# Two Newton halves moved from the opening of an audio tower into its token groups

## What is computed

```python
fr = jnp.fft.rfft(xp, axis=-1)
feats = jnp.concatenate([jnp.abs(fr), jnp.angle(fr)], axis=-1)
h = jax.nn.gelu(feats @ W1 + b1, approximate=False) @ W2 + b2

inv_term = jnp.linalg.inv(I - 0.5 * dt * A)        # 32 x 32
A_bar = (I + 0.5 * dt * A) @ inv_term
# scan: state = tanh(state @ A_bar.T + ub_t)        (state space layer, on layernorm(h))
# scan: z, r, c gates; h_new = z * h + (1 - z) * c  (recurrence, 256 wide, 320 steps)
```

## Time and profile before

| | us |
|---|---|
| median of 3 runs | 890.94 |
| lowest, highest | 890.02, 891.04 |
| the profiled execution | 889.93 |
| its span | 888.1 |
| PE busy | 831.7 (94%) |
| DVE busy | 583.0 (66%) |
| ACT busy | 370.9 (42%) |
| POOL busy | 74.5 (8%) |
| half clock on TensorE in the front | 54.0 to 67.65 |

### The profile page before, as it was taken

How to read it: one execution, slowest core, us unless ns; L and a number is a source line. 1 busy time by engine, 2 the same in 40 slices (tenths; PEclk the granted TensorE clock), 3 DMA queues, 4 the chain that set the end, 5 groups by cost and what they waited for, 6 DMA issues and landing times.

```text
span 888.1 us, 40652 instructions
## 1 busy us (share of the span) xinstructions
PE 831.7 (94%) x17111; PEld 704.6 (79%) x17111; DVE 583.0 (66%) x3495; ACT 370.9 (42%) x2016; POOL 74.5 (8%) x189
## 2 busy tenths in 40 slices
PE   8999999989999999999999999999999998988875
PEld 7677667778888888888888888888888887877765
DVE  5343538376777776767767777777677777676655
ACT  5565766433343443433434434334334343343322
POOL 3111102110000000100000001000000000000000
PEclk9979999955555555555555555555555555555555
DMA  7100000000000000000000000000000000000000
GB/s 172 38 1 0 1 1 1 2 3 3 7 3 6 7 3 6 7 3 6 4 6 7 3 6 7 3 6 4 7 6 4 6 7 3 6 6 3 7 3 8
DMA packets 7454, 8.53 MB, mean 10 GB/s; under 512 B 1343, under 2 KB 6557, under 8 KB 7271
## 3 DMA queue, kind: packets, MB, share of 16 engines
q1 hardware_dynamic: 6965, 5.92, 2.9%
q0 software_dynamic: 256, 0.01, 0.0%
q10 hardware_dynamic: 50, 0.00, 0.0%
HBM read 4.62 MB, written 1.31 MB: 7 GB/s over the span
## 4 chain that ended last, share of the span: by engine, by line
PE 85%; ACT 7%; DVE 4%; issue 3%; POOL 0%; POOLq 0%; DVEq 0%
PE ps L1527 42%; PE ps L1533 11%; PE ps L1340 8%; PE ps L1238 4%; PE ps L1440 3%; PE ps L1541 3%; PE ps L1404 3%; DVE h_hi L479 2%; PE ps L1448 2%; ACT addend L847 1%; PE ps L1322 1%; PE ps L1329 1%; PE ps L1310 1%; PE ps L1260 1%; PE ps L1254 1%
## 5 line engine op out<-in xcount | busy, mean ns | idle before, releaser
L1527 PE MATMUL ps<-h_hi,w_first 128*128 128x8 f16 x2552 | 267.6, 170 | 27.8 <-DVE h_hi L479 27.7
L1527 PEld LDWEIGHTS ps<-h_hi,w_first 128*128 128x128 f16 x2552 | 220.3, 104 | 89.8 <-DVE h_hi L479 89.8
L1527 PE MATMUL ps<-h_hi,w_rest 128*128 128x8 f16 x5104 | 275.8, 168 | 0.0
L1527 PEld LDWEIGHTS ps<-h_hi,w_rest 128*128 128x128 bf16 x5104 | 241.0, 105 | 0.1
L837 ACT ACTIVATE tanh_r<-ps 128x16 f32<-128x16 f32 x320 | 59.2, 185 | 250.2 <-PE ps L1533 249.7
L1533 PE MATMUL ps<-h_lo,w_first 128*128 128x8 f16 x2560 | 159.0, 168 | 0.1
L1527 PE MATMUL ps<-rh_hi,w_first 128*128 128x8 f16 x1276 | 136.0, 172 | 12.6 <-DVE rh_hi L1132 0.9
L1527 PEld LDWEIGHTS ps<-rh_hi,w_first 128*128 128x128 f16 x1276 | 109.0, 104 | 39.6 <-DVE rh_hi L1132 1.1
L1527 PE MATMUL ps<-rh_hi,w_rest 128*128 128x8 f16 x2552 | 138.6, 168 | 0.0
L479 DVE TENSOR_TENSOR_SCAN h_hi<-coef,addend 128x32 f16<-128x32 f32 x320 | 73.3, 229 | 83.7 <-ACT addend L847 83.7
L1527 PEld LDWEIGHTS ps<-rh_hi,w_rest 128*128 128x128 bf16 x2552 | 121.2, 105 | 0.0
(11 more groups left out here) (210 smaller groups left out, 1375.3 us busy)
## 6 DMA issues: line engine op xcount, KB each, us to landing
x_sb<-in_x SPq DMA_DIRECT2D x4, 500.0 KB
out<-res SPq DMA_DIRECT2D x20, 64.0 KB, 2.0
W_sb<-in_L_tok_W SPq DMA_DIRECT2D x1, 606.0 KB
W_sb<-in_L_tok_W SPq DMA_DIRECT2D x1, 384.0 KB
wnat<-in_L_ffn_Wwr SPq DMA_DIRECT2D x1, 256.0 KB, 5.5
wnat<-in_L_ffn_Wwz SPq DMA_DIRECT2D x1, 256.0 KB, 11.8
wnat<-in_L_ffn_Ww SPq DMA_DIRECT2D x1, 256.0 KB, 10.4
wunat<-in_L_ffn_Wur SPq DMA_DIRECT2D x1, 128.0 KB, 7.1
```

Source lines behind the costliest of these rows:

```text
L1527: mm(gate(c, j, g, m), w[:, m * 128:(m + 1) * 128], state[:, k * NB:(k + 1) * NB], start=False, stop=False, skip_group_check=True)
```

## The change

`EARLY` goes from 8 to 6: halves 6 and 7 leave the opening, and with them 24 fillers. `WARM` goes from 52 to 47. The places are dealt anew: the first place of groups 0 and 1, (0, 0, 0) and (1, 0, 0), is left free, and in groups 1 and 3 slot 1 of the last two pieces is used. The wait for the second imaginary part, which the loop of the opening had, moves to the half in place (0, 0, 1). From group 4 on each half stands where it stood.

```diff
-WARM = 52
+WARM = 47
 BUSY = 6
-EARLY = 8
+EARLY = 6
...
         def blocked(n, m, slot):
-            if slot == 1 and n % 2:
+            if slot == 1 and n % 2 and (n > 3 or m < MC - 2):
                 return True
...
-            if (n, m, slot) in ((0, SQRT_PIECE + 2, 1), (2, SQRT_PIECE + 1, 1), (4, SQRT_PIECE + 1, 1)):
+            if (n, m, slot) in ((0, 0, 0), (1, 0, 0), (0, SQRT_PIECE + 2, 1), (2, SQRT_PIECE + 1, 1), (4, SQRT_PIECE + 1, 1)):
                 return True
...
             a.activation(biasT[:], bank(6)[:, 0:32], ACT.Copy).then_inc(su_act, 1)
-            for i in range(6, EARLY):
-                newton(i)
...
             tr(bank(6)[:, 0:32], bias_rows[:], ident[0:32, 0:32]).then_inc(bias_psum, 1)
-            for i in range(6, EARLY):
-                if i == 6:
-                    pe.wait_ge(im_read, 2)
-                busy(2 * BUSY if i == 6 else BUSY, 7)
-                newton(i)
-            busy(BUSY, 7)
             pe.wait_ge(w1_in, 32)
...
                     i = SLOTS[n, m, slot]
+                    if (n, m, slot) == (0, 0, 1):
+                        pe.wait_ge(im_read, 2)
```

## The result

The changed kernel took 887.46 us in the median of six runs (887.05 to 887.83), the kernel before beside it 891.01 (890.02 to 892.71): a ratio of 0.9957, 95% interval 0.9945 to 0.9968. It is faster by 3.6 us, 0.4%, where 9.6 from the median were forecast. The range held the time, by 0.04 us and only because it reached to rival 2; the sum behind the forecast did not come out.

The account below looks back on a forecast made before the run. PE was taken to bound the front, through needless work, waits and lower clock. Terms -0.55 - 3.12 - 1.33 - 5.37 + 1.2 = -9.2 gave 880.7 from the profile, 881.8 from the median; forecast 881.3, range 879.0 to 887.5.

Parts of the forecast that it names:

- rival 2: A lower-clock stretch remains, at group 1's head, its table-load wait or the opening: 886.1 or 886.7 us; chance 0.26.
- (d): Group 1: with the 1.48 us wait cut to about 0.5, the clock stays up; -5.37 us, bounds 0 and -5.9.
- (b): Opening's end: 24 fillers and halves 6 and 7 go, first angle product starts earlier; -3.12 us, bounds -2.6 and -3.2.
- The third place: Group 1's wait for the table loads, 1.13 us by group 3, named as a place where the clock could fall.
- (a): Program start: five fillers fewer, so first patch transposes start earlier; -0.55 us, bounds 0 and -0.69.
- (c): Group 1's head: Newton place left free, so the output product starts with its gelu; -1.33 us, wait 0.4 to 0.6 left.
- The twin: Group 3, same products as group 1 at full clock: 15.81 us against 21.18, used to price the lower clock.
- (e): Ends of groups 1 and 3: four more Newton halves at 0.30 each; +1.2 us, bounds 0.8 and 2.8.
- Rival 3: Clock falls at group 1's table-load wait and doesn't come back soon: +23, some 904 us; chance 0.08.
- Rival 4: Two lower-clock stretches of the old length: 891.4 us, no change; chance 0.05.
- Rival 5: Opening: something the fillers hid makes PE wait, so the start and opening gains come back: 884.4 us; chance 0.07.
- a stretch at 0.50 ahead of 160 us: Half granted clock anywhere ahead of 160 us; the prediction named this as showing it wrong.

Follow-up runs that it names:

- e5: The changed kernel itself, measured again with nothing altered, on another chip: 885.26 us, 0.9937 of the kernel before.
- e3: Changed kernel with the Newton place at group 1's head taken again and the added place at that group's sixth piece free; short opening stays: 887.04 us, 0.9975.
- e4: Changed kernel with the 52 warm-up transposes of the kernel before instead of 47, nothing else: 883.82 us, 0.9935.
- e8: Changed kernel with three and four fillers in the opening's later waits for halves 7 and 8, the bias-column wait left empty: 883.44 us, 0.9926.
- e14: Changed kernel with four fillers in the 0.54 us wait at group 1's head, opening's wait left empty, run once more: 882.66 us, 0.9929.
- e2: Kernel before with only the Newton place at group 1's head freed, one place at that group's last piece taken for it: 882.82 us, 0.9923.
- e1: Changed kernel with eight filler transposes in the opening's 0.93 us wait for the bias columns: 881.84 us, 0.9913.
- e16: Kernel before with twelve fillers in the 1.48 us wait at group 1's head, no place moved: 884.84 us, 0.9947.
- e13: Changed kernel with eight fillers in the opening's bias-column wait and four in the wait at group 1's head: 882.32 us, 0.9919.
- e15: The changed kernel itself, measured a fourth time with nothing altered: 885.09 us, 0.9945 of the kernel before.
- e6: Changed kernel with eight fillers and half 6 in the opening's bias-column wait, the added place at group 1's sixth piece free again: 882.62 us, 0.9913.
- e11: Changed kernel with four fillers in the 0.54 us wait at group 1's head, opening's wait left empty: 882.73 us, 0.9917.
- e10: Changed kernel with eight fillers in the opening's bias-column wait, the same kernel as e1 run again: 883.38 us, 0.9932.
- e12: The changed kernel itself, measured a third time with nothing altered: 885.84 us, 0.9953 of the kernel before.

## Why the prediction came out wrong

**The step that failed** is the last sentence of (d)'s first half, "So I take it that the clock stays up", together with the cover in (b). (b) priced what the fillers and halves 6 and 7 had covered as 1.19 us of waiting that costs nothing, and put no price on an empty PE. (d) then looked for the one place as empty as the 1.48, found 1.13 and 0.88 without a fall in one profile, and took that for safe. The same opening with a wait of 0.93 fell in three of the changed kernel's four profiles and held in the fourth, e5, and in e3, e4, e8 and e14; the wait of about 0.5 at group 1's head, which (d) took as harmless, fell in e5 (0.53) and held in the ten other profiles that have it, e2 and e4 among them. So at these lengths a fall is no property of the wait alone: it comes in some executions and not in others, and one profile shows one of them. Behind the 1.48 it looks certain: all 47 executions of the kernel before beside e1 to e16 have a mean clock of 0.591 to 0.593, that of its profile. Rival 2, with two of its three places named rightly, is what happened, at 886.1 to 886.7 forecast and 887.46, 885.26, 885.84 and 885.09 measured; it deserved more than 0.26. That the range held the time is this rival's doing, and luck: its lower end, 879.0, is not the sum that it names, which gives 889.93 - 10.18 = 879.75. The third place, the wait behind the arctangents (0.78 to 0.93 in group 1, 1.13 in group 3), fell in no profile.

The sizes, by steps:

- (a) five fillers fewer, -0.55 forecast. -0.69 in the first pair of profiles, but that can't be put down to the change. With 52 warm-up transposes the first patch transposes start at 9.59, 8.74, 9.65 and 9.17 (before, e2, e4, e16), 9.29 in the mean; with 47 at 8.90 to 9.75 in fourteen profiles, 9.29 in the mean. A late rise of the clock makes the same warm-up longer (rise at 5.30, patch transposes at 8.90; at 7.67, 9.75), and with an early one PE waits for DVE's odd halves (0.92 in e5, to 9.33). The lower bound, 0, was right, for other reasons.
- (b) -3.12 forecast, -3.03 from the first patch transposes to the first angle product (in e4 -3.12). The rows of the bias columns carried it: from the bias transpose to the first angle product 2.65 was forecast and 2.66 measured; PE's idle part of it was 0.93, not 1.19.
- (c) -1.33 forecast, -1.31 measured, with the wait of 0.54 that was forecast at 0.4 to 0.6.
- (d) -5.37 forecast. By e16, which has group 1 as before and at full clock, 21.18 - 16.44 = -4.74. The twin was not quite one. Group 1's wait behind the arctangents is 0.78, not group 3's 1.13; and in group 1 the even half stands ahead of the angle product and in group 3 the odd one, so a piece takes 2.03 in the one (e16, group 1, the first three rows) and 1.79 in the other (the kernel before, group 3):

```profile
55.80 0.65 PE L1238 MATMUL ps<-magT,W_sb 101*128 101x256 f32 x2
56.45 0.41 PE L1254 MATMUL ps<-Xn,step_w 128*128 128x32 f32 x2
...
57.83 0.65 PE L1238 MATMUL ps<-magT,W_sb 101*128 101x256 f32 x2
...
99.65 0.68 PE L1238 MATMUL ps<-magT,W_sb 101*128 101x256 f32 x2
100.17 0.36 PE L1256 MATMUL ps<-DY 128*128 128x64 f32 x2
...
101.44 0.68 PE L1238 MATMUL ps<-magT,W_sb 101*128 101x256 f32 x2
```

- (e) +1.2 forecast; 17.17 - 16.44 = 0.73 in group 1, 16.54 - 15.81 = 0.73 in group 3, and 0.22 in the rest of group 0, which no term had: +1.68, inside its bounds.

With these sizes and no fall the sum is -3.03 - 1.31 - 4.74 + 1.68 = -7.4, and e4, whose profile has no fall, shows it: 157.76 from the first patch transposes to the first `tanh_r`, against 165.26 before, -7.50. From a kernel before at 889.8 to 891.1 this is 882.3 to 883.7; the fastest execution of the changed kernel on each of the three later chips is 882.12, 882.94 and 883.63 (the last with 3.41 us at half clock). The rest is the falls: in the changed kernel's profiles that way takes 162.32, 161.41, 161.00 and 159.59, so 4.6, 3.7, 3.2 and 1.8 above e4's 157.76. The -3.6 of the first pair of profiles is -7.5 for the change, +4.6 for a fall and -0.7 from the warm-up.

Rival 3 (a fall that stays) has no trace: the changed kernel's stretches ended after 10.24 us at most. Rival 4 (two stretches) is not seen in any profile of the changed kernel. Rival 5 (a wait that the fillers hid) did not occur: PE waits for the bias columns and nothing else. The section of the Trainium skill that names long waits for a DMA ("TensorE: Matmul & The Clock Gate", "HAM oscillation — how this bites in real kernels") would have had another cause for the fall at 54.0. The runs here differ: PE waits for ACT in that place, for 1.48 us, at a DMA share of 0.01 behind it, and filling the wait (e16) or cutting it to 0.53 (e2) is enough.

Of the signs that the prediction named, a stretch at 0.50 ahead of 160 us came, and told rightly. It also said that it would be wrong if the recurrence changed its length by more than 1 us. It did, by 1.6, and this was a poor sign to name: that length moves by up to 3.4 us from execution to execution.

## What to carry to other kernels

Filler work that looks free to remove may be what keeps the clock up: before taking it out, ask what PE does in its place, and where the answer is "wait", leave fillers in the wait, where they cost nothing (here twelve short transposes in two waits were worth 2.8 us, e13 against e15). Read a fall of the clock behind a short wait as a chance and not as a property of the wait: take several profiles and each execution's mean granted clock before a stretch is called safe, and close all the places of a kind: on one chip the executions went from 881.04 to 881.80 with nearly all filled and from 882.12 to 888.63 without. A second group with the same products is a fair price for a clock stretch only if its small steps stand in the same order and its waits are as long.

## What the runs showed of the hardware

- The clock fell behind waits for ACT of 0.93 and 0.53 us in some executions of one program and not in others. In three profiles (e6, e11, e16) it fell near 19 us, behind a wait for DVE of 0.30 to 0.45 and one for ACT of 0.37 or 0.38; e10 has 0.41 and 0.37 there and no fall. It never fell, in the profiles here, behind the 1.13 in group 3 or the 0.78 to 0.93 in group 1. The length of the wait alone does not order them.
- The clock's first rise in the warm-up came between 4.38 and 7.67 us of the span, for one program too (4.83 and 7.67 in e11 and e14). With the same 47 fillers the first patch transposes start at 8.90 to 9.75. Of the nine profiles with the rise at 5.50 or earlier six have a fall ahead of 50 us (the first of the changed kernel, e6, e11, e12, e15, e16); of the nine with the rise at 6.18 or later none has. The kernels differ, and no run sets the instant of the rise, so the cause of this order is not shown.
- At the lower clock PE was busy throughout in some stretches (13.65 of 13.65 us in e3, 10.24 of 10.24 in e5), and yet the stretches lasted 3.41, 6.83, 10.24 or 13.65 us.
- The recurrence, the same 16 thousand products in each kernel, at 1.2 GHz but for its first 1.3 to 4.5 us, took 705.50 (e2) to 708.90 us (e12) from its first `tanh_r` to its last. No run here shows why; it is nearly as large as the effect first measured.
